# Five slots with the pair's second FFN product ahead of the shared bank's use, four with the tanh between two exponentials

## What is computed

```python
q, k, v = heads(x @ Wq + bq), heads(x @ Wk + bk), heads(x @ Wv + bv)      # x layer-normed
y  = softmax(causal(q k^T * scale)) v
y += softmax(qc kc^T * scale) vc          # qc from x, kc and vc from a 64-channel context
x  = x + (y @ Wp + bp)
xf = layernorm(x)
shared = silu(xf @ shared_w1.T) * (xf @ shared_w2.T) @ shared_w3.T         # 512 wide
gates  = sigmoid(xf @ router_w.T) where the biased score is in the top 2 of 8, else 0
h      = silu(h1) * h2 * gates            # h1, h2 from w12, eight experts of 128
out    = x + shared + sum over experts of h @ w3
```

## Time and profile before

| what | value |
|---|---|
| median of 3 runs | 432.44 us |
| the three runs | 429.89, 432.44, 443.41 us |
| the profiled execution | 430.54 us |
| its span, first to last instruction | 428.8 us |
| granted PE clock, mean | 0.998 |
| PE / DVE / ACT / POOL busy in the span | 384.5 / 352.8 / 196.1 / 77.6 us |

### The profile page before, as it was taken

One profiled execution on the slowest core, in us unless ns is written; L12 is line 12 of the kernel. 1 busy time (PEld: TensorE's weight loads), 2 busy tenths in 40 slices (PEclk: granted clock), 3 DMA queues, 4 the chain that ended last, 5 costly groups with the idle time before them and its releaser, 6 DMA issues.

```text
span 428.8 us, 10370 instructions
## 1 busy us (share of the span) xinstructions
PE 384.5 (90%) x3724; PEld 287.9 (67%) x3724; DVE 352.8 (82%) x1186; ACT 196.1 (46%) x326; POOL 77.6 (18%) x140
## 2 busy tenths in 40 slices
PE   1569999989999999999999999999999999998986
PEld 0446666667677767767677767767677767765985
DVE  4486777778989789888989799888989698984877
ACT  5124654554444553554444553455444644355221
POOL 5012101412131103202131103202131103201210
PEclk9999999999999999999999999999999999999999
DMA  5731202110201111110200111110200110000000
GB/s 133 212 103 44 68 9 89 49 45 2 88 19 39 50 44 43 55 49 0 86 20 35 49 46 40 55 49 0 75 27 31 44 44 33 2 26 0 2 14 12
DMA packets 28478, 19.63 MB, mean 46 GB/s; under 512 B 6680, under 2 KB 26272, under 8 KB 28448
## 3 DMA queue, kind: packets, MB, share of 16 engines
q1 hardware_dynamic: 27296, 19.02, 13.7%
q10 hardware_dynamic: 1152, 0.20, 0.4%
HBM read 5.58 MB, written 1.05 MB: 15 GB/s over the span
## 4 chain that ended last, share of the span: by engine, by line
PE 45%; DVE 34%; ACT 9%; issue 8%; DMA 2%; SPq 1%; DVEq 0%; ACTq 0%
DVE masked_s L1053 10%; PE Bk L438 8%; PE Y L586 8%; PE Cb L438 6%; ACT probs L813 5%; DVE act L934 4%; DVE shifts L1059 4%; PE S L462 4%; PE A L438 4%; DVE acc L974 3%; PE Y L553 3%; PE S L480 2%; DVE qs L1026 2%; DVE hid L943 2%; PE Cb L669 2%
## 5 line engine op out<-in xcount | busy, mean ns | idle before, releaser
L813 ACT ACTIVATE probs<-S 128x1024 f32<-128x1024 f32 (+1 forms) x128 | 111.6, 917 | 45.8 <-PE S L464 44.8
L1053 DVE CUSTOM_DVE_ANT_0 masked_s<-S,later_keys 128x256 f32<-128x256 f32 (+1 forms) x256 | 74.1, 353 | 5.2 <-PE S L476 5.0
L1059 DVE TENSOR_REDUCE shifts<-S 128x4 f32<-128x1024 f32 x64 | 75.4, 1218 | 0.9 <-PE S L480 0.5
L800 ACT COPY yT<-Y 128x256 f32<-128x256 f32 x64 | 23.8, 372 | 113.7 <-PE Y L586 113.7
L586 PE MATMUL Y<-probs,vs 128*32 128x256 f32 (+1 forms) x1024 | 62.4, 362 | 5.2 <-DVE qs L1026 3.1
L1109 POOL TENSOR_SCALAR_AFFINE_SELECT probs<-probs 128x1024 f32<-128x1024 f32 x32 | 35.2, 1099 | 151.6 <-ACT probs L813 151.6
L462 PE MATMUL S<-qs,qk 32*128 32x256 f32 x256 | 44.3, 387 | 7.9 <-DVE shifts L1053 5.4
L438 PEld LDWEIGHTS Bk<-w3T,hid 128*128 128x128 f32 x336 | 40.7, 191 | 12.8 <-DVE hid L943 12.0
L438 PE MATMUL Bk<-w3T,hid 128*128 128x128 f32 x336 | 48.5, 287 | 0.6 <-DVE hid L943 0.6
L586 PEld LDWEIGHTS Y<-probs,vs 128*32 128x32 f32 x1024 | 26.9, 110 | 27.7 <-DVE qs L1026 12.5
L934 DVE SCALAR_TENSOR_TENSOR act<-th,A 128x512 f32<-128x512 f32 x42 | 28.6, 681 | 16.2 <-ACT th L793 15.2
(11 more groups left out here) (149 smaller groups left out, 671.3 us busy)
## 6 DMA issues: line engine op xcount, KB each, us to landing
qk<-nat SPq DMA_DIRECT2D x192, 64.0 KB, 1.9
xin<-in_x_dram SPq DMA_DIRECT2D x8, 128.0 KB, 2.3
w_raw<-in_L_ffn_w_dram SPq DMA_DIRECT2D x4, 256.0 KB
xres<-in_x_dram SPq DMA_DIRECT2D x8, 128.0 KB, 2.3
out_dram<-acc SPq DMA_DIRECT2D x8, 128.0 KB, 1.8
cin<-in_ctx_dram SPq DMA_DIRECT2D x8, 64.0 KB, 2.0
w_raw<-in_L_ffn_shared_w_dram SPq DMA_DIRECT2D x4, 128.0 KB
w_raw<-in_L_ffn_w_dram SPq DMA_DIRECT2D x1, 512.0 KB
```

The source lines that it names most:

```text
L813: nc.scalar.activation(probs[s % 2][:, hs, 0:kept(s)], S[:, hs, 0:kept(s)], ACT.Exp, scale=SCALE).then_inc(exped[s], 1)
L1053: r_ = nc.vector.tensor_tensor_reduce(out=masked_s[:, j, T - q * T:T - q * T + keys], in0=S[:, j, T - q * T:T - q * T + keys], in1=later_k ...
L1059: nc.vector.tensor_reduce(dst.rearrange("p q j -> p j q"), S[:, hs, :].rearrange("p j (q k) -> p j q k", q=NT), AX_X, ALU.max).then_inc(re ...
```

## The change

No instruction is added or dropped. Three queues are reordered:

- PE: in the pair slots 0, 1, 2, 3 and 5 h2 stands ahead of the EARLY use of Cb (xT, tokens3, yT, vc, v). Slot 6 (qkc) stays as it was.
- ACT: in slots 1, 2, 3 and 6, where there is both a unit and an h1, tanh stands between the exponentials of half 0 and half 1 and no longer behind both.
- DVE: the reading of tokens3 and vc (slots 1 and 3) stands behind `activate` and ahead of `qs`; that of v (slot 5) behind `qs` and `times_h2`, directly ahead of the reductions. xT's in slot 0 stays behind `times_h2`.

```diff
@@ PE, one_turn
                     if pair_of(s):
                         if h1_of(s) and turn.has(h1_of(s)[1]):
                             hidden(turn, h1_of(s), 0)
-                        if turn.at(1) and s == 2:
-
-                            fill(Bk, 3)
-                        bank_c(turn, EARLY[s])
+                        if s == 6:
+                            bank_c(turn, EARLY[s])
                         if turn.has(pair_of(s)[1]):
                             hidden(turn, pair_of(s), 1)
+                        if turn.at(1) and s == 2:
+
+                            fill(Bk, 3)
+                        if s != 6:
+                            bank_c(turn, EARLY[s])
                         shift_rows(turn, s)
@@ ACT
+            def h1_between(turn, s):
+
+                return s in (1, 2, 3, 6) and turn.has(0) and turn.has(h1_of(s)[1])
...
                             nc.scalar.activation(probs[s % 2][:, hs, 0:kept(s)], S[:, hs, 0:kept(s)], ACT.Exp,
                                                  scale=SCALE).then_inc(exped[s], 1)
-                    if h1_of(s) and turn.has(h1_of(s)[1]):
+                            if half == 0 and h1_between(turn, s):
+                                tanh_h1(turn, h1_of(s))
+                    if h1_of(s) and turn.has(h1_of(s)[1]) and not h1_between(turn, s):
                         tanh_h1(turn, h1_of(s))
@@ DVE, one_turn
                 for s in range(SLOTS):
-                    late = EARLY[s] and EARLY[s][0] in ("xT", "qkc", "tokens0")
-                    if not late:
-                        from_bank_c(turn, EARLY[s])
...
                         activate(turn, pr)
+                    if s in (1, 3):
+                        from_bank_c(turn, EARLY[s])
...
                         times_h2(turn, pr)
-                    if late and s not in (6, 7):
+                    if s in (0, 5):
                         from_bank_c(turn, EARLY[s])
```

More of the change, by code:

```diff
@@ L693, in one_turn @@
                             hidden(turn, h1_of(s), 0)
+                        if s == 6:
+                            bank_c(turn, EARLY[s])
+                        if turn.has(pair_of(s)[1]):
+                            hidden(turn, pair_of(s), 1)
                         if turn.at(1) and s == 2:
                             fill(Bk, 3)
-                        bank_c(turn, EARLY[s])
-                        if turn.has(pair_of(s)[1]):
-                            hidden(turn, pair_of(s), 1)
+                        if s != 6:
+                            bank_c(turn, EARLY[s])
                         shift_rows(turn, s)
```

## The result

The changed kernel takes 424.49 us in the median of 4 runs (423.79 to 424.79), the kernel before 431.21 in the median of its 4. The ratio is 0.9855 with a 95% interval of 0.9819 to 0.9892: faster by 1.5%, inside the 2% band to which the prediction had given 0.85. Every ratio in this document leaves out runs over 1.5% above the fastest of their own kernel, as 443.41 us is here. Forecast were 426.0 us, 1.0% under the profiled execution of before; measured is 1.4% (424.66 against 430.54 in the two profiled executions). The span fell from 428.8 to 422.9 us.

A forecast was written before the change was run, and what follows sets the result against it. PE and DVE, both nearly full, wait for each other in turns. Gains of 0.67 us in four turns (2.7), 1.0 each in turns 6 and 7 and -0.1 in turn 1 make 4.5 us off 430.54: 426.0, range 420.5 to 431.

The forecast's parts named there:

- 2% band: Whole kernel: about 2% (8.6 us) tells a change from no change; a result within it got 0.85.
- Slot 0: h2 fills PE's 0.5 us wait before xT; act limits qs's gain to 0.13 us, 0.43 in turn 6.
- Slot 1: tanh stays bound by h1, tokens3 is read behind act; gain 0.05 us, between -0.05 and 0.11.
- Slot 2: Earlier tanh and h2 ahead of yT bring qs 0.59 us sooner; up to 0.1 may stay with PE.
- three signs: Wrong if: slot 6's products start earlier than explained; second exponential holds back maxima (slots 1 to 3); h2 waits for acc.
- Slot 3: vc and its reading come later, tanh gains nothing, qs stays about where it was: gain 0.
- Slots 5 and 6: Slot 5: v's uncovered reading loses 0.1 us. Slot 6: tanh wait goes, but PE's shift rows hold qs, gain 0.
- the rival by which DVE's gaps count in full: DVE's aimed-at gaps all close, 4.1 us in each of six turns: 24.6 us, 405.9 us; chance 0.03.
- Turn 7: Slot 6 has no qkc there, so tanh ahead of one exponential gains 0.9 us; turn total 1.0.
- All of PE's gaps counting: PE's 1.4 us of gaps close in six turns, plus 0.9: 9.3 us, 421.2 us; chance 0.14.
- Gains waited for again: Half of slot 2's gain lost, slot 5 costs 0.3, a turn gives 0.2: 429 to 430 us; chance 0.14.
- The slower case: Reads of vc and v cost 0.40 us each in slots 3 and 5: 432.6 us; chance 0.09.

The follow-up runs named there:

- order alone: Changed kernel with tanh back behind both exponentials, so only PE's and DVE's reordering: ratio to before 0.9981 (ten more runs), turn 47.73 us.
- Tanh alone: Kernel before with only ACT's edit, tanh between the exponentials in slots 1, 2, 3 and 6: ratio to before 0.9971, turn 48.01 us.
- slot 2 alone: Kernel before with h2 ahead of yT and tanh between the exponentials, in slot 2 only: ratio 0.9971, turn 47.50 us.
- the fill: Changed kernel with three extra matmuls that nobody reads ahead of slot 6's shift-row transposes: turn 47.53 us, where the changed kernel takes 47.16.
- the fill in slot 0: Changed kernel with the same three unread matmuls ahead of slot 0's shift-row transposes instead of slot 6's: turn 47.16 us.

## Why the prediction came out right

**Slot 0, 0.13 and 0.43 in turn 6:** 0.13 and 0.50 measured. `qs` is bound by `act` now, as worked out. Turn 2, which I took for a turn like 3 to 5, gained 0.44 (6.15 to 5.71 us), as turn 6 did. In turns 3 to 5 DVE idles 0.33 to 0.36 us ahead of `act` ("issue" in the earlier trace rows); in turn 2 it doesn't, so before the change `qs` there waited for PE:

```profile
113.66 0.42 DVE L1026 TENSOR_TENSOR qs<-qk,Y 128x256 fp32r<-128x256 f32 x1 [0.36 <-PE Y L553]
```

**Slot 1, 0.05, between -0.05 and 0.11:** 0.18 measured, outside my bounds. This term was mis-sized, for two reasons the rows show: h2 is 0.1 us shorter directly behind h1, and the modelled ends of the matmuls, from which I took the later of two values, lie 0.1 to 0.2 us behind the point where the next group starts (h1 ends at 212.56 + 0.28 = 212.84 by its row, and h2 starts at 212.69). The order alone gives this gain (6.73 us), so tanh has no part in it, as predicted.

**Slot 2, 0.59 with both parts needed:** 0.61, of which 0.07 are given back in slot 3. Tanh alone and order alone leave it at 6.52 us, both in this slot alone bring 5.93: shown. That the second exponential would be there when PE reaches the maxima was 0.3 us too hopeful. This is one of the three signs by which the prediction wanted to be called wrong, and it came, though at a price of only 0.07 us a turn; the other two didn't.

**Slot 3, 0:** 0 by the place of vc; the 0.07 us that it loses come from slot 2.

**Slots 5 and 6, -0.1 and 0:** `qs` of slot 5 gains 0.36 and that of slot 6 loses 0.37. From the `qs` of slot 4 to the reductions of slot 5 it is 6.37 us against 6.33 before: the uncovered reading costs what the order brings, with -0.04 where I had -0.1. Slot 6 was bound by PE's shift rows, as the wait of 0.70 us and the fill show. That its tanh wait would go away nearly whole was wrong, 0.62 of 1.35 us stayed, but cost nothing, since `qs` waited behind it anyway. The fill also answers the rival by which DVE's gaps count in full, at 405.9 us: PE has room in the turn, as in slot 0, but not at this place.

**Turn 7, 0.9 in slot 6:** 0.91.

**The sum** was 4.5 us and is 5.9. From one turn's `qs` of slot 7 to the next, turns 2 to 5 gained 1.12, 0.77, 0.84 and 0.79 us where I had 0.67 each, the first of them with slot 0's extra 0.3; turn 6 gained 1.25 instead of 1.0 and turn 7 1.00 as forecast, and 0.15 us were lost by the end of turn 1, where I had 0.1. Together that is 5.6 us, by which the last `qs` of turn 7 is earlier (389.09 - 383.47). The remaining 0.3 us come in the drain, which takes 37.8 to 39.8 us from that `qs` in the profiles of this case (39.7 before, 39.4 after), so I can't ascribe them to the change. The forecast was near because its largest terms were right, slot 2 and turn 7; what was too small was slot 1's term and turn 2's slot 0.

**The rivals.** All of PE's gaps counting (421.2) was nearest on the fast side; 3.5 us were missing. PE's four gaps did close, but 0.3 us a turn came back as a longer wait of `values` for `qs` (0.5 against 0.2 us), and 0.3 in the maxima that are held up and count as busy. Gains waited for again: no wait of h2 for `acc` appears; the rival's own sum, with turn 7's 0.9 in it, is 428.4 and not 429 to 430. The slower case was right on slot 5, where the reading is on the path. In slot 3 the reading of vc waits only 0.20 us, and PE's shift rows, which start at 226.91 us and take 0.44, would hold `qs` until about 227.39 (by the 0.04 us in the earlier trace rows), against 227.42 with the reading: an estimate by which it costs next to nothing. Forecasting against the profiled execution and not against the median was sound: before's fourth run was 429.97.

## What to carry to other kernels

Where two full queues release each other, ask at each joint which of the two is there last, and cost an edit only up to the other one: in slot 2 two edits that were each worth nothing alone were worth 0.53 us a turn together. A wait that disappears from one row and turns up under another name in the next (`act` for tanh, then `qs` for the shift rows) names the next edit; following it here gave 1.2 us a turn on top of 0.8 to 0.9, in all 3.2% under the kernel before. To learn whether an engine is the bound at a place, put a little idle work there and at a second place, and compare; the answer holds for the turns that were compared.

## What the runs showed that I had not expected

In these profiles the spread of the times sits mostly in one stretch. Between 44 and 48 us the granted clock was 1.00 in the changed kernel's profile and 0.70 in that of the fill in slot 0, and PE got through 44 and 35 matmuls:

```profile
44.00:48.00 4.00, 4.00 (x44) 2.50 (x42) 3.45 (x6) 1.56 (x4) 1.10 (x1) 1.00 0.27 98
```

```profile
44.00:48.00 4.00, 4.00 (x35) 2.42 (x34) 3.17 (x5) 0.69 (x2) 1.10 (x1) 0.70 0.28 102
```

0.70 is a mixture of the upper level, 2.4 GHz, and the lower, 1.2. PE was busy for 4.00 of the 4.00 us before this in both. What tips it is open. The stretch from the `qs` at 33 us to the third one after it took 15.4 us in the changed kernel, 17.2 in the fill in slot 0 and 21.8 in the profile of slot 2 alone; there a pair of score matmuls took 0.58 us at 45 us instead of 0.39, and four matmuls of the maxima 0.80 us at 48.72 instead of 0.50, although the granted clock stands at 1.00 in both windows. The same four took 0.80 us at 98.75 us in the first profile of the order alone, and there the granted clock is 0.53 from 98 to 100 us, nearly the lower level. So by its matmuls PE ran near the lower level at 45 to 49 us too, and the record of the clock doesn't show it: to learn the clock of a stretch, compare matmuls of the same shape. A second such stretch lies between 90 and 113 us and cost up to 3.7 us in these profiles. A difference of up to 6 us between two single runs of this kernel can therefore be the first stretch and nothing of the edit; the length of a later turn, read from two rows of one profile, told 0.1 us apart.

A product of six matmuls takes PE 0.71 us behind another of the same shape and 0.80 us behind transposes or 64-row products (the rows of slot 6, and 215.28 to 216.08 us in slot 1 before): in these rows a change of shape costs about 0.1 us, at the first pair of matmuls (0.50 against 0.40 us in slot 6).
